# A macaron transformer layer on one core: the first iteration's feed-forward pieces spread over more steps, the fourth tile's input in another buffer, two norms moved from VectorE to GpSimd

## What is computed

```python
def _L0_ffn_ref(x, k0, k1, k2, s0, s1, s2):
    h = jnp.concatenate([x, -x], axis=-1)
    h = s0 * _conn_dense(k0, h)          # w = where(k, 1, -1); 256 -> 512
    h = jax.nn.relu(h) * 2
    h = s1 * _conn_dense(k1, h)          # 512 -> 512
    h = jax.nn.relu(h) * 2
    h = s2 * _conn_dense(k2, h)          # 512 -> 128
    return h
...
x = x + 0.5 * _L0_ffn_ref(_layernorm(x, axis=-1), ...)
x = x + _L0_attn_ref(_layernorm(x, axis=-1), ...)   # ends in its own layernorm with gamma, beta
x = x + 0.5 * _L0_ffn_ref(_layernorm(x, axis=-1), ...)
```

## Time and profile before

| what | value |
|---|---|
| time, median of 3 runs | 772.38 us (767.18 to 772.47) |
| the profiled execution | 771.31 us, its span 769.0 us |
| busy share of the span | PE 91%, DVE 84%, ACT 66%, POOL 47% |
| mean granted TensorE clock | 0.969 of full speed |
| chain that ended last, by engine | PE 54%, DVE 23%, ACT 4% |

### The profile page before, as it was taken

The page is one execution under the profiler, slowest core; times in us unless marked ns, Lnnn a source line. Parts: engine busy times, 40 slices in busy tenths (PEclk is TensorE's granted clock), DMA queues, the critical chain, the costliest instruction groups (busy, mean ns, idle before and its releaser), DMA issues.

```text
span 769.0 us, 18471 instructions
## 1 busy us (share of the span) xinstructions
...
## 2 busy tenths in 40 slices
PE   7778696999999999999999999999999998887878
...
DVE  6686787898989989898989999898989997777765
...
PEclk9898797999999999999999999999999999899998
...
GB/s 79 49 8 29 36 43 23 29 43 11 64 16 64 16 64 17 42 37 2 64 15 64 17 64 16 43 36 3 65 15 64 16 50 17 29 38 2 16 1 27
DMA packets 29508, 25.62 MB, mean 33 GB/s; under 512 B 4336, under 2 KB 29424, under 8 KB 29424
## 3 DMA queue, kind: packets, MB, share of 16 engines
...
q10 hardware_dynamic: 1760, 0.85, 0.4%
...
HBM read 5.05 MB, written 4.19 MB: 12 GB/s over the span
## 4 chain that ended last, share of the span: by engine, by line
PE 54%; DVE 23%; ACT 4%; issue 2%; POOL 2%; POOLq 0%; DVEq 0%
DVE row_max L1408 11%; PE ps_z L675 11%; PE ps_z L676 10%; PE ps_c L840 8%; PE ps_s L789 7%; DVE ffn_lo L1287 6%; PE ps_m L763 3%; PE ps_m L852 2%; PE ps_z L657 2%; PE ps_z L686 2%; ACT probs L1070 2%; PE ps_z L688 2%; PE ps_m L774 2%; ACT ffn_hi L1032 1%; DVE k_lo L1399 1%
## 5 line engine op out<-in xcount | busy, mean ns | idle before, releaser
L1408 DVE TENSOR_REDUCE row_max<-ps_s 128x4 f32<-128x1024 f32 x256 | 312.1, 1219 | 58.1 <-PE ps_s L789 57.4
L1070 ACT ACTIVATE probs<-ps_t,score_scale 128x1024 f32<-128x1024 f32 x252 | 280.1, 1112 | 71.7 <-PE ps_t L802 69.4
L1032 ACT ACTIVATE ffn_hi<-ps_z 128x512 f16<-128x512 f32 x261 | 149.6, 595 | 85.4 <-PE ps_z L676 69.9
L675 PE MATMUL ps_z<-ffn_hi,w 128*128 128x512 f16 x464 | 178.1, 384 | 0.1
L676 PE MATMUL ps_z<-ffn_lo,w 128*128 128x512 f16 x464 | 177.0, 381 | 0.0
L1287 DVE SCALAR_TENSOR_TENSOR ffn_lo<-ps_z,ffn_hi 128x512 f16<-128x512 f32 x232 | 155.4, 680 | 9.0 <-ACT ffn_hi L1032 7.3
L840 PE MATMUL ps_c<-probs,v_cols 128*32 128x256 f32 x2048 | 134.3, 391 | 1.3 <-ACT probs L1070 0.7
L789 PE MATMUL ps_s<-k_rows,q_rows 32*128 32x256 f16 x1024 | 102.2, 278 | 27.9 <-DVE row_max L1408 27.4
L802 PE MATMUL ps_t<-q_rows,k_rows 32*128 32x256 f16 x992 | 98.6, 277 | 0.0
L840 PEld LDWEIGHTS ps_c<-probs,v_cols 128*32 128x32 f32 x2048 | 57.7, 111 | 55.9 <-issue 29.0
L789 PEld LDWEIGHTS ps_s<-k_rows,q_rows 32*128 32x128 f16 x1024 | 29.1, 92 | 119.3 <-DVE row_max L1408 59.6
...
## 6 DMA issues: line engine op xcount, KB each, us to landing
...
q_rows<-q_hi SPq DMA_DIRECT2D x32, 128.0 KB, 2.5
...
k_rows<-k_hi SPq DMA_DIRECT2D x30, 128.0 KB, 2.1
q_rows<-no_max SPq DMA_DIRECT2D x16, 128.0 KB, 2.1
q_rows<-q_lo SPq DMA_DIRECT2D x16, 128.0 KB, 2.1
k_rows<-k_lo SPq DMA_DIRECT2D x15, 128.0 KB, 2.1
q_rows<-max_rows SPq DMA_DIRECT2D x64, 8.0 KB
```

Source lines behind the costliest of these rows:

```text
L675: pe.matmul(o[:], w, ffn_hi[:, 1 + k, :], start=(k == 0), stop=False)
L1032: a_.activation(ffn_hi[:, use, :], ps_z[use % 2][:], ACT.Relu if use else ACT.Copy, scale=1.0 if use else XN_SCALE).then_inc(z_hi, 1)
L1070: a_.activation(probs[n % PROBS][:, j:j + 2, :], o[:], ACT.Exp, scale=score_scale[:, 0:1]).then_inc(s_exp, 1)
L1408: v.tensor_reduce(row_max[hb % 2][:].rearrange("p (a l) e -> p l a e", a=2)[:, j:j + 2, :, g % 2], ps_s[:].rearrange("p l (a k) -> p l a k ...
```

## The change

1. The pieces of tile 2's feed-forward step stand at 6 + piece * 21 // 15, which is steps 6, 7, 8, 10, 11, 13, 14, 15, 17, 18, 20, 21, 22, 24, 25, 27. LNT, Q, K and V of tile 1 move to steps 13, 16, 20 and 23, and K of iteration 0 uses the bank `ps_c`.
2. Tile 3 is loaded into `x3` as soon as tile 1's residual has been made, and its statistics stand at steps 20 and 23. Tile 4 is loaded into `x0` at the end of iteration 0, and its statistics at steps 8 and 10 of iteration 1 instead of 20 and 21.
3. GpSimd applies the three norms that DVE applied.
4. In the head, one of three DMAs of tile 0's keys goes from ACT's queue to SP's.

```diff
-PACE_ZERO = {6 + piece: piece for piece in range(PIECES)}
+PACE_ZERO = {6 + piece * 21 // 15: piece for piece in range(PIECES)}
-AT_ZERO = {"LNT": 12, "Q": 15, "K": 18, "V": 22}
+AT_ZERO = {"LNT": 13, "Q": 16, "K": 20, "V": 23}
-AT_STATS_B_ZERO, AT_STATS_PREP_ZERO = ((26,) * TT, 27), ((28, 28, 30, 30), 31)
+AT_STATS_B_ZERO, AT_STATS_PREP_ZERO = ((20, 20, 23, 23), 24), ((28, 28, 30, 30), 31)
-AT_NORM_NEXT_ZERO, AFTER_STATS_B, AT_NORM_A_ALONE = 10, (3, 4), (7, 5)
-AT_STATS_B_ONE = ((20, 20, 21, 21), 22)
+AT_NORM_A_ALONE = (7, 5)
+AT_STATS_B_ONE = ((8, 8, 10, 10), 11)
...
 # SP, head and steps
             spread(0, 2, PARTS)
+            sp.wait_ge(s_kfill[0], 1)
+            sp.wait_ge(m_hi, 3)
+            spread(0, SPREADS - 1, SPREADS)
...
                 if not it.prev:
+                    sp.wait_ge(z_free, Z_USES)
+                    sp.dma_start(x3[:].rearrange("p (b a) d -> p b a d", b=2),
+                                 tile_rows(x_flat, start_of(3))).then_inc(s_tile1, 16)
                     place_max(t, par, 0)
                     place_max(t, par, 1)
                     sp.wait_ge(m_free, it.misc["K"] + 1)
                     spread(1 - par, 0, SPREADS)
-                if it.next_b is not None:
+                if it.next_b is not None and not it.first:
                     start = start_of(t + 3)
...
                     place_max(t, par, 2)
+                if not it.prev:
+                    sp.wait_ge(z_free, Z_USES * (it.ffn_b + 1))
+                    load_x(start_of(4))
...
 # GpSimd, steps
                 if not it.prev:
-                    att_deviation(t + 1)
+                    att_norm(t + 1, 1 - par)
+                elif it.first:
+                    ffn_norm(it.next_b, x0)
...
-                    if it.next_b is not None and it.vector_b and it.prev:
-                        ffn_deviation(it.next_b)
...
-                elif it.next_b is not None and not it.prev:
-                    ffn_deviation(it.next_b)
+                elif not it.prev:
+                    ffn_norm(it.next_b, x3)
...
 # PE, project and steps (ACT's and DVE's halves likewise)
                 if o is ps_m:
                     misc_wait(use)
+                else:
+                    at_least(pe, mt_free, last_max["c"])
...
-                            project(1, it.misc["K"])
+                            project(1, it.misc["K"], ps_m if it.prev else ps_c)
...
 # ACT, head
-                    for part in (0, 2):
-                        a_.dma_start(k_rows[0][part::SLOTS, :, :], qk_hi[1][:]).then_inc(s_spread, 16)
+                    a_.dma_start(k_rows[0][0::SLOTS, :, :], qk_hi[1][:]).then_inc(s_spread, 16)
...
 # DVE, steps
-                    if it.vector_b and s == stats_b[1] + AFTER_STATS_B[t]:
-                        ffn_apply(it.next_b, x0)
-                    if not it.prev and s == AT_NORM_NEXT_ZERO:
-                        att_apply(1, 1)
```

More of the change, by code:

```diff
@@ L103, in __init__ @@
         self.stats_a = cur and ffn_a is not None
-        self.vector_b = t <= 1
+        self.first = t == 0 or t == 1
         self.at = AT_OWN_LAST if own_contexts else AT_ZERO if not prev else AT_ALONE if pace else AT
@@ L234, in macaron_layer @@
         s_norm_in = sem("gamma_beta_bv_loaded")
-        s_tile1 = sem("tile1_loaded")
+        s_tile1 = sem("tiles_1_3_loaded")
         s_x0 = sem("x0_loaded")
@@ L334, in at_stats_b @@
         def at_stats_b(it):
-            return AT_STATS_B_ZERO if not it.prev else AT_STATS_B_ONE if it.vector_b else AT_STATS_B
+            return AT_STATS_B_ZERO if not it.prev else AT_STATS_B_ONE if it.first else AT_STATS_B
         def at_stats_prep(it):
@@ L628, in steps @@
                     split_max(t, 2)
-                if it.next_b is not None and not it.vector_b:
+                if it.next_b is not None and not it.first:
                     ffn_norm(it.next_b, x0)
-                elif it.next_b is not None and not it.prev:
-                    ffn_deviation(it.next_b)
+                elif not it.prev:
+                    ffn_norm(it.next_b, x3)
                 if it.prev:
@@ L1148, in steps @@
                         if s == at(it, "K"):
-                            qk_split(1, it.misc["K"])
+                            qk_split(1, it.misc["K"], ps_m if it.prev else ps_c)
             run(act, steps)
@@ L1503, in steps @@
                             ffn_piece(f, piece, x3, x1[1])
+                        elif it.first and it.prev:
+                            ffn_piece(f, piece, x3, x1[par], based=t + 1)
                         else:
@@ L1534, in steps @@
                         if s - 1 == at(it, "K"):
-                            qk_rest(t + 1, 1)
+                            qk_rest(t + 1, 1, ps_m if it.prev else ps_c)
                     if it.pace and it.stats_a and s == AT_NORM_A_ALONE[it.own_contexts]:
                         ffn_apply(it.ffn_a, x2[par])
-                    if it.vector_b and s == stats_b[1] + AFTER_STATS_B[t]:
-                        ffn_apply(it.next_b, x0)
-                    if not it.prev and s == AT_NORM_NEXT_ZERO:
-                        att_apply(1, 1)
                     if not it.prev and s == AT_STATS_NEXT_ZERO[1]:
```

6 lines of the change are left out of this document (4 added, 2 removed).

## The result

The changed kernel takes 764.14 us in the median of 7 runs (760.58 to 766.21), the kernel before 769.82 (766.72 to 772.47, 7 runs). The ratio is 0.9913, with a 95% interval of 0.9887 to 0.9939: it is faster by 5.7 us or 0.9%, within the 1% that the prediction set as its bound. The forecast was 765.0. The profiled executions stand at 764.67 and 771.31, spans 762.5 and 769.0, which is 6.6 us between them. A span is the time from the first to the last instruction of the profiled execution.

A forecast was written before the change was run, and what follows sets the result against it. Iteration 0 was taken as bound by PE and DVE taking turns at one buffer, steady iterations by PE. -6.3 - 1.4 + 0.8 + 0.6 = -6.3 from 771.31 gave 765.0 us, likeliest 763.5 to 767.5, 8-in-10 range 760.5 to 769.5.

The forecast's parts named there:

- the replay: Iterations 0 and 1 recomputed with the new instruction lists from profiled prices: -6.3 us and -1.4 us.
- the slip: Allowance for small gaps a replay leaves out, a tenth of iteration 0's gain: +0.6 us.
- s6 to s12: Iteration 0, DVE-bound: att_xn and one ffn_lo leave DVE (1.7 us), a wait for ACT adds 0.3: -1.4 us.
- s12 to s16: Iteration 0, PE-bound: fewer pieces before s16, GpSimd's att_xn in time, clock low as long as before: -0.9 us.
- s16 to s20: Iteration 0: less PE work and no 1.57 us wait, as K comes later and in ps_c: -2.5 us.
- s20 to s26: Iteration 0: pieces 10 to 13, K and V arrive here, 7.5 us against 6.64: +0.9 us.
- s26 to iteration 1: End of iteration 0, DVE-bound: tile 3's input wait, statistics and norm leave, 5.75 against 8.18: -2.4 us.
- iteration 0: Sum of the five stretches of iteration 0: -6.3 us, to 38.6 us.
- iteration 1: DVE loses tile 4's statistics, norm and one aggregate from s20 on; statistics at s8 and s10 cost 0: -1.4 us.
- The clock: Low clock lasts further into iteration 1, 1.6 us more dense work under it: +0.8 us, ends -1.2 and +2.
- The price: Cost of the low clock: half a microsecond for each one at 1.2 GHz under dense PE work.
- The rival that the clock would turn the whole into a loss: Low clock begins sooner in steps 6 to 14, a second lies over iteration 1: 773 to 780 us; chance 0.06.

The follow-up runs named there:

- e12: The kernel before with extra matmuls that nobody reads, more than e6 at s29 and s31 of iteration 0 and s27 of iteration 1: 760.22 us.
- e5: The changed kernel with extra matmuls that nobody reads in iterations 0, 1, 14 and 15, in the head and at the end: 752.71 us.
- e8: The changed kernel with the extra matmuls of e5, but DVE applies the three norms again: 755.7 us.
- e1: The changed kernel with the spreading undone (tile 2's pieces at steps 6 to 21; LNT, Q, K, V at 12, 15, 18, 22): 769.6 us.
- e3: The changed kernel with K of iteration 0 back in the bank ps_m, nothing else: 765.11 us in one run.
- e11: The kernel of e5 with tile 4's statistics and aggregate back at steps 20 to 22 of iteration 1, its norm still on GpSimd: 756.7 us.
- e2: The changed kernel with the three norms given back to DVE, no extra matmuls: 763.94 us.
- e6: The kernel before with extra matmuls that nobody reads, in iteration 0 at steps 7, 9, 11 and odd steps from 23, elsewhere as in e5: 763.11 us.
- e7: The kernel of e5 with the spreading undone as in e1 and iteration 0's extra matmuls as in e6: 756.39 us.
- e4: The kernel before with only the new steps of pieces and LNT, Q, K, V, and tile 3's statistics at s29: 770.36 us.

## Why the prediction was right, and where its steps were wrong

The time was forecast at 765.0 (likeliest case 763.5 to 767.5) and is 764.1. Between the profiled executions, from which the sum was made, -6.3 was forecast and -6.6 measured; between the medians -7.4 and -5.7, since the median of before fell from 772.38 (3 runs) to 769.82 (7 runs). That the sum is so close is in part luck: iterations 0 and 1 gave 8.2 us where the replay less the slip had 7.1, and 1.6 were lost at a lower clock in the head and in iterations 2 and 14 where 0.8 was set for iteration 1. The starts of `row_max` that it named, 55.9, 62.4, 67.0, 74.5 and 80.3, came at 57.06, 63.03, 67.48, 75.01 and 80.52. The mechanism stands: what bound iteration 0 was the turn of PE and DVE at `ps_s` and whatever one of them did beside it, and the change moved that beside the other's work. Step by step:

| stretch | predicted | measured | with the clock held (e12, e5) |
|---|---|---|---|
| s6 to s12 | -1.4 | 7.90 - 8.44 = -0.5 | 6.82 - 8.43 = -1.6 |
| s12 to s16 | -0.9 | 5.97 - 7.43 = -1.5 | 4.81 - 4.84 = 0.0 |
| s16 to s20 | -2.5 | 4.45 - 7.14 = -2.7 | 4.69 - 7.14 = -2.5 |
| s20 to s26 | +0.9 | 7.53 - 6.64 = +0.9 | 7.33 - 6.64 = +0.7 |
| s26 to iteration 1 | -2.4 | 5.51 - 8.18 = -2.7 | 5.51 - 8.01 = -2.5 |
| iteration 0 | -6.3 | -6.5 | -5.9 |
| iteration 1 | -1.4 | -1.7 | -1.3 |

**s6 to s12.** The instructions that left DVE were counted rightly, as the column with the held clock shows, though the 1.0 us that `att_xn` gives this stretch is lost again in the next (e8). Two things made it -0.5. The completions of the pieces wait for ACT twice, not once, 0.90 us instead of 0.3:

```profile
55.17 0.69 DVE L1297 SCALAR_TENSOR_TENSOR ffn_lo<-ps_z,ffn_hi 128x512 f16<-128x512 f32 x1 [0.31 <-ACT ffn_hi L1043]
...
56.45 0.69 DVE L1297 SCALAR_TENSOR_TENSOR ffn_lo<-ps_z,ffn_hi 128x512 f16<-128x512 f32 x1 [0.59 <-ACT ffn_hi L1043]
```

And the clock fell at 52.3, not at 55.1, and stayed low up to 62.5: 10.2 us at 1.2 GHz where the means of the earlier trace rows make 2 x (0.13 x 8.44 + 0.31 x 7.43) = 6.8 before. Part of ACT's lateness is PE's at that clock: with the clock held, the stretch has neither loss.

**s12 to s16.** The step said "with the clock low for as long as before". That was wrong in length, 2 x 0.46 x 5.97 = 5.5 us where it had been 2 x 0.31 x 7.43 = 4.6, and the sum of the first two stretches (-2.0 for -2.3) came out by luck. At the full clock both kernels need the same for this stretch, 4.84 and 4.81 us. The pieces moved out of it did shorten it, to 3.87 in e8, as the step says (-0.9); but with `att_xn` on GpSimd the stretch starts 1.0 us sooner and the norm is not there sooner: in e5 PE waits 0.37 us for it, and DVE 1.25 us at 55.92 for the copy by ACT of what PE made behind it. So over both stretches the change is worth 1.6 us at the full clock, not 2.3, and the step that counted `att_xn`'s leaving as a gain of its own was wrong. The 1.5 us measured here are the clock's: it costs the stretch 1.2 us now and cost it 2.6 before, when it lay over 34 matmuls instead of 27. `att_xn` came at 56.52, 0.3 later than computed, and PE waited 0.34 us for it:

```profile
55.48 1.04 POOL L519 TENSOR_TENSOR att_xn<-att_xc,att_rs 128x512 f32<-128x512 f32 x1
...
56.67 1.09 PE L761 MATMUL ps_m<-ident,att_xn 128*128 128x128 f32 x4 [0.34 <-POOL att_xn L519]
```

**s16 to s20.** The size is right, and the wait of the earlier trace rows is gone:

```profile
66.06 0.28 PE L876 MATMUL ps_m<-ident,max_parts 128*16 128x128 f16 x2
66.86 0.28 PE L800 MATMUL ps_s<-k_rows,q_rows 32*128 32x256 f16 x2 [0.52 <-DVE row_max L1418]
```

But the reason named two things, "K comes later and in `ps_c`", and only the first acts (e1, e3). The transpose waits for a count of finished uses, and K raises that count in whichever bank it stands; a transpose ahead of K in the order doesn't ask for it.

**s20 to s26** and **s26 to the end** are as computed. PE is full for 7.53 of 7.53 us, the three turns at the end stand nearly alone (DVE 5.31 of 5.51 us), no wait of DVE for a DMA is left, and the last DMA of tile 1's spread goes out at 75.41, ahead of the scores that need it. The aggregate of tile 3 came later than I had it, the norm began at 74.47 instead of 73.6, and had time to spare all the same: its last instruction starts at 76.71.

```profile
76.71 1.04 POOL L519 TENSOR_TENSOR ffn_xn<-ffn_xc,ffn_rs 128x512 f32<-128x512 f32 x1
```

**Iteration 1.** Statistics at s8 and s10 at cost 0: right, by the halves of e8 and e12. For what they free later I had 0.6 and 0.2, and the halves show 0.85. The norm I had at 0.6; it is 0.37 (e8). GpSimd's norm ahead of `att_y` ends at 101.40 and `att_y` starts at 103.39 once DVE's part is there, so it delays nothing, as computed.

**The norms on GpSimd.** All three norms moved (the title counts two). Together they are worth 1.06 + 0.37 = 1.4 us, tile 3's and tile 4's; the attention norm's move is worth nothing (e8). That comes at about twice the busy time on their new engine (GpSimd's in iteration 0 is 8.91 us against 5.03, DVE's 32.39 against 34.41). "GPSIMD Engine Reference", section "Engine selection", of the Trainium skill gives about twice the time for two-input elementwise operations on GpSimd and would keep them on VectorE. The rows agree with it on the duration and not on the choice: here it was a gain, since GpSimd was idle for most of iteration 0 and the two norms that pay are there before PE wants them; the third, for which PE waited 0.34 us, pays nothing. e11 shows the condition. The same norm behind later statistics delays three small instructions that PE waits for, and costs 2.0 us at once.

**The clock.** The term was +0.8 with ends of -1.2 and +2. Its sign holds, its place does not. With the clock held the change is worth 7.5 us, without it 5.7 in the medians, so the clock takes back 1.8 (1.3 between the profiled spans), about twice the term and within its ends. It was to come from a longer half clock at the start of iteration 1. There it got shorter, 3.4 us from 79.6 to 83.0, while the 0.53 of the earlier trace rows and the 0.94 of the earlier trace rows make 2 x (0.47 x 8.18 + 0.06 x 23.25) = 10.5 before. Against their partners with the clock held, iterations 0 and 1 of the changed kernel lose 2.2 and 0.7 us, those of before 2.8 and 1.1. So there the clock gives 1.0 us back. The loss is in other places: 0.6 more each in the head, in iteration 2 (2.2 against 1.5) and in iteration 14, and 0.3 more in iteration 15 and the end. Of these only the head was edited, by one DMA. The time at 1.2 GHz did not grow: both profiled executions have a mean clock of 0.969, which is 2 x 0.031 of the span, 47 to 48 us each. What differs is the work that lies under it. In iteration 2, the same code each time, the mean clock is 0.97 in e2, 0.96 before, and 0.94 in the changed kernel and in e1, and it takes 44.73, 45.12, 45.77 and 45.91 us, against 43.60 at 1.00. Iteration 14 has 0.88 where it had 0.92. What sets the moment of a fall is not settled, and e2 and e1 show that it is not these iterations' own code. The price was off too: the prediction took half a microsecond for each one at 1.2 GHz from iteration 2's 2.12 us above iteration 3, but 0.6 of those remain at the full clock, which leaves 1.5 for 3.6, or 0.4.

The rival that the clock would turn the whole into a loss began as it said, with an earlier fall in s6 to s12, but PE came back at 62.5, before s16, and the second low stretch was short. The slip was sized well: with the clock held, iterations 0 and 1 give 7.2 of the 7.7 us that the replay had, 0.5 less where 0.6 was set.

"TensorE: Matmul & The Clock Gate", section "HAM oscillation", of the Trainium skill says that gaps throttle PE and that the work behind them starts cold. The runs agree: more work at s7 to s12 and s28 to s31 kept the clock at 1.00, and e12 against e6 shows the same boundary without and with a fall, by 17 more matmuls ahead of it.

**The parts.** Of iteration 0's 5.9 us with the clock held, the spreading makes 3.5 (e7), tile 3's norm 1.1 (e8), and the rest, 1.35, is what is left for tile 3's early input and statistics. That part was not run by itself, and neither was the DMA moved in the head. The parts need each other: spreading alone came to nothing (e4), since DVE then waits 1.22 us for tile 3's input, PE 2.23 us for its norm, and iteration 1 runs at a lower clock.
